# Another hand-written order for a two-layer attention and feed-forward kernel

## The reference, cut to what matters

```python
x = x + L0_xattn(layernorm(x), ctx)   # A: 16 heads of 16, softmax over 77 keys, output projection
x = x + L0_ffn(layernorm(x))          # B: 256 -> 1024 -> 256, ReLU; expert 0 alone counts; inner layernorm Y
x = x + L1_xattn(layernorm(x), ctx)   # C: one head of 256, softmax over 77 keys
x = x + L1_ffn(layernorm(x))          # D: token s goes through matrix W[idx[s]], idx = argmax of a table of 8 scores
...
idx = argmax(einsum('sp,tp->st', pe, sign(tile_sigs)))
out = take_along_axis(einsum('bsd,tod->bsto', x, W) + b, idx)
```

## Time and profile before

| | |
|---|---|
| median of the timed runs | 274.63 us (3 runs, 273.89 to 274.74) |
| span of the profiled execution, first to last instruction | 272.0 us |
| median less that span: what lies around the span | 2.6 us |
| PE busy | 249.2 us, 92% |
| DVE / POOL / ACT busy | 220.3 / 189.7 / 160.7 us |
| PE in the chain that ended last | 68% |
| mean granted TensorE clock | 0.982 of full speed |

### The profile page before, as it was taken

One profiled execution on the slowest core, in us unless ns is written; L12 is line 12 of the kernel. 1 busy time (PEld: TensorE's weight loads), 2 busy tenths in 40 slices (PEclk: granted clock), 3 DMA queues, 4 the chain that ended last, 5 costly groups with the idle time before them and its releaser, 6 DMA issues.

```text
span 272.0 us, 6214 instructions
## 1 busy us (share of the span) xinstructions
PE 249.2 (92%) x2048; PEld 221.2 (81%) x2048; DVE 220.3 (81%) x573; ACT 160.7 (59%) x510; POOL 189.7 (70%) x361
## 2 busy tenths in 40 slices
...
GB/s 175 329 326 89 0 81 0 2 39 42 39 2 40 41 265 86 14 9 2 0 2 63 76 77 42 58 60 40 57 217 2 0 0 2 0 2 2 39 154 116
DMA packets 11156, 17.61 MB, mean 65 GB/s; under 512 B 1377, under 2 KB 7509, under 8 KB 11125
## 3 DMA queue, kind: packets, MB, share of 16 engines
...
...
## 4 chain that ended last, share of the span: by engine, by line
PE 68%; DVE 15%; POOL 5%; ACT 5%; issue 4%; DMA 1%; SPq 0%; POOLq 0%; DVEq 0%; ACTq 0%
PE PB L266 29%; PE PB L259 12%; PE PB L464 9%; PE S L387 5%; PE PB L339 5%; PE PB L399 4%; PE S L377 4%; ACT E L1066 2%; DVE SX L659 2%; POOL E L1263 1%; DMA WKV<-in_w_k 1%; DVE SX L673 1%; POOL SM L1220 1%; DVE HL L686 1%; DVE XTL L638 1%
## 5 line engine op out<-in xcount | busy, mean ns | idle before, releaser
L1263 POOL TENSOR_TENSOR E<-E,SX 128x308 f32<-128x308 f32 x64 | 43.8, 712 | 10.7 <-DVE SX L676 10.4
L1066 ACT ACTIVATE E<-S,SX 128x77 f32<-128x77 f32 x128 | 39.4, 336 | 10.6 <-DVE SX L659 10.6
L266 PE MATMUL PB<-XTH,W1H 128*128 128x256 f32 x128 | 37.7, 295 | 1.5 <-DVE XTL L638 1.4
L266 PE MATMUL PB<-W2H,HH 128*128 128x256 f32 x128 | 37.6, 294 | 0.0
L266 PE MATMUL PB<-XTL,W1H 128*128 128x256 f32 x128 | 36.2, 283 | 0.0
L266 PE MATMUL PB<-XTH,W1L 128*128 128x256 f32 x128 | 36.2, 282 | 0.0
L266 PE MATMUL PB<-W2H,HL 128*128 128x256 f32 x128 | 35.5, 278 | 0.0
L266 PE MATMUL PB<-W2L,HH 128*128 128x256 f32 x128 | 35.5, 278 | 0.0
L1220 POOL TENSOR_TENSOR SM<-SM,nhalf 128x2 f32<-128x2 f32 x40 | 28.3, 707 | 3.1
L1089 ACT ACTIVATE HH<-PB 128x512 fp32r<-128x512 f32 x32 | 19.0, 598 | 18.0 <-PE PB L266 18.0
L1076 ACT ACTIVATE EW<-S 124x640 f32<-124x640 f32 x32 | 21.9, 711 | 10.9 <-PE S L387 10.1
...
## 6 DMA issues: line engine op xcount, KB each, us to landing
...
```

The source lines that it names most:

```text
L266: t = e.matmul(dst, a, b, start=first and j == 0, stop=last and j == n - 1)
L1066: t = e.activation(Ei[:, h * NK:(h + 1) * NK], P[:, at:at + NK], ACT.Exp, bias=SX[:, i, 0, k:k + 1], accum_out=SX[:, i, 1, k:k + 1])
L1263: t = e.tensor_tensor(Eh, Eh, SX[:, i, 2, 8 * a + h:8 * a + h + 4].unsqueeze(2).to_broadcast([128, 4, NK]), ALU.mult)
```

## The change

All four lists are written anew and most PSUM banks are other ones. The steps themselves, 246 on PE, 274 on DVE, 218 on ACT and 142 on POOL, are the same, with the same operations and waits; SP's list is untouched. The diff below is cut to the places that the text comes to. In the lists, `r_pairs` and the registers' `starts` stand later, `pivot` on DVE stands later, and `sx(1)` on POOL stands ahead of `en(6, 1, 1)`.

```diff
# PE
-            sc(2, 1, 0, 1); sc(2, 1, 1, 0); pv(1, 1); r_perm(1); w1(0, 0, 3); wo(1, 0); w1(0, 1, 2); w1(0, 2, 1)
-            w1(0, 3, 3); f_m(0); tE(2, 0, 0, 0); tA(3, 2); w2(0, 0, 0, 1); tE(2, 0, 1, 1); tB(1, 0); w2(0, 0, 1)
-            w2(0, 1, 0); q(3, 2); w2(0, 1, 1); w1(1, 0, 3); sc(3, 0, 0, 1); sc(3, 0, 1, 0); w1(1, 1, 0); w1(1, 2, 2)
...
-            cp(1, 3); cs(2, 0); tE(5, 1, 0, 1); tE(5, 1, 1, 0); co(1); pv(5, 0, 2); pv(5, 1); sc(6, 0, 0, 1)
-            sc(6, 0, 1, 0); wo(5, 2); tC(3, 0); tB(4, 3); sc(6, 1, 0, 0); q(7, 1); sc(6, 1, 1, 1); cp(2, 3); cs(3, 2)
-            co(2); w1(4, 0, 1); w1(4, 1, 0); w1(4, 2, 3); w1(4, 3, 2); cp(3, 1); tE(6, 0, 0, 1); tE(6, 0, 1, 0)
-            w2(4, 0, 0, 3); tB(5, 0); co(3); sc(7, 0, 0, 0); sc(7, 0, 1, 1); w2(4, 0, 1); w2(4, 1, 0); w2(4, 1, 1)
-            w1(5, 0, 1); w1(5, 1, 0); tE(6, 1, 0, 0); w1(5, 2, 2); tE(6, 1, 1, 1); w1(5, 3, 3); sc(7, 1, 0, 1)
...
-            pr(0, 0, 2); w2(6, 0, 0, 1); cp(4, 0); w2(6, 0, 1); tB(7, 3); co(4); w2(6, 1, 0); tC(5, 0); w2(6, 1, 1)
-            cs(5, 3); w1(7, 0, 2); tD(2, 1); w1(7, 1, 3); w1(7, 2, 0); w1(7, 3, 1); cp(5, 3); w2(7, 0, 0, 2); co(5)
-            tD(3, 0); w2(7, 0, 1); w2(7, 1, 0); w2(7, 1, 1); tC(6, 0); tD(4, 3); pr(0, 1, 1); cs(6, 2); pr(0, 2, 3)
...
+            tB(0, 0); wo(1, 1); sc(3, 0, 0, 1); w1(0, 0, 0); w1(0, 1, 2); f_c(); w1(0, 2, 0); w1(0, 3, 1)
+            tE(2, 0, 1, 0); w2(0, 0, 0, 2); sc(3, 0, 1, 0); sc(3, 1, 0, 1); w2(0, 0, 1); tB(1, 0); w2(0, 1, 0)
+            w2(0, 1, 1); tE(2, 1, 0, 0); w1(1, 0, 0); tA(4, 1); tE(2, 1, 1, 0); w1(1, 1, 3); sc(3, 1, 1, 0)
...
+            tA(6, 2); sc(5, 0, 0, 0); sc(5, 0, 1, 1); w2(2, 0, 0, 3); q(6, 1); cp(0, 2); w2(2, 0, 1); tE(4, 0, 1, 0)
+            w2(2, 1, 0); w2(2, 1, 1); tE(4, 1, 0, 0); tC(1, 1); co(0); tB(3, 0); tE(4, 1, 1, 1); cs(1, 3)
...
+            sc(7, 0, 0, 0); sc(7, 0, 1, 1); tC(3, 0); co(1); w2(4, 0, 1); cs(3, 0); cp(2, 1); tB(5, 3); w2(4, 1, 0)
+            tE(6, 0, 1, 0); cp(3, 3); co(2); co(3); w2(4, 1, 1); w1(5, 0, 1); tE(6, 1, 0, 1); w1(5, 1, 0)
+            tE(6, 1, 1, 1); pv(6, 0, 2); pv(6, 1); sc(7, 1, 0, 0); sc(7, 1, 1, 1); w1(5, 2, 3); wo(6, 1)
+            w1(5, 3, 0); tE(7, 0, 0, 1); w2(5, 0, 0, 2); tE(7, 0, 1, 1); w2(5, 0, 1); w2(5, 1, 0); w2(5, 1, 1)
...
+            w1(7, 1, 0); w1(7, 2, 2); cp(5, 1); w1(7, 3, 3); w2(7, 0, 0, 0); co(5); w2(7, 0, 1); w2(7, 1, 0)
+            w2(7, 1, 1); tD(3, 2); tC(6, 3); pr(0, 0, 1); tD(4, 3); cs(6, 2); pr(0, 1, 0); pr(0, 2, 3); cp(6, 2)
# DVE
-            hl(0, 3); apply("B", 1); lo("A", 3); r_pairs(); lo("B", 1); ssum(2, 1, 1); ql(3); y(0); stats("A", 4)
...
-            smax(5, 0, 0); ssum(4, 0, 1); lo("B", 3); ssum(4, 1, 0); cm(0); ssum(4, 1, 1); apply("C", 1); starts()
...
+            smax(2, 1, 0); smax(2, 1, 1); lo("B", 0); r_index(); ssum(2, 0, 1); f_q(); hl(0, 0); smax(3, 0, 0)
+            x1(1); ssum(2, 1, 0); hl(0, 1); kbl(1); stats("B", 1); stats("A", 4); hl(0, 2); hl(0, 3); apply("B", 1)
+            stats("A", 5); ssum(2, 1, 1); smax(3, 0, 1); ssum(3, 0, 0); smax(3, 1, 0); lo("B", 1); apply("A", 4)
...
+            hl(1, 2); ssum(3, 0, 1); apply("C", 0); ssum(3, 1, 0); hl(1, 3); ql(4); r_pairs(); ssum(3, 1, 1)
...
+            lo("A", 6); smax(5, 0, 0); hl(2, 3); ssum(4, 1, 0); stats("A", 7); ssum(4, 1, 1); stats("B", 3); ql(6)
+            starts(); apply("B", 3); apply("C", 1); smax(5, 0, 1); y(2); ssum(5, 0, 0); stats("Y", 2); apply("A", 7)
...
+            ssum(6, 1, 1); x3_(1); apply("B", 5); ssum(7, 0, 0); cm(3); lo("B", 5); x3_(2); smax(7, 0, 1); x3_(3)
# ACT
-            starts(); hi("A", 4); o(2); ex(3, 1, 0); ex(3, 1, 1); apply("C", 0); et(3, 0, 0); apply("A", 5)
...
+            hh(4, 2); hh(4, 3); starts(); ex(6, 1, 1); apply("B", 5); xtc(3); ex(7, 0, 0); hi("B", 5); cex(3)
# POOL
-            be(4); b2(4); bs(4); bs(5); en(6, 0, 0); rs("B", 5); bo(7); en(6, 0, 1); bs(6); bs(7); en(6, 1, 0); b2(5)
-            en(6, 1, 1); be(5); sx(0); rs("Y", 4); sx(1); rs("C", 4); rs("D", 0); sx(3); en(7, 0, 0); en(7, 0, 1)
...
+            rs("Y", 3); bo(6); rs("C", 3); b2(4); be(4); en(6, 0, 1); rs("B", 5); bs(6); en(6, 1, 0); one(5); sx(1)
+            bo(7); b2(5); en(6, 1, 1); en(7, 0, 0); be(5); sx(0); rs("Y", 4); sx(2); sx(3); one(6); en(7, 0, 1)
```

More of the change, by code:

```diff
@@ L532, in tensor @@
[L532 to L536, removed]
@@ L958, in f_o @@
                                 .to_broadcast([NK, 2, 256]), ALU.add).then_inc(s["d_f"], 1)
[L960 to L963, removed]
@@ L969, in vector @@
[L969 to L973, removed]
@@ L979, in vector @@
[L979 to L988, removed]
@@ L989, in vector @@
-            apply("D", 4); y(7); stats("Y", 7); x2(7); stats("C", 7); cm(6); pa(0, 1); apply("C", 7); pa(0, 2)
-            apply("D", 5); pa(0, 3); cm(7); x3_(6); stats("D", 6); x3_(7); apply("D", 6); stats("D", 7); apply("D", 7)
-            pa(1, 0); pa(1, 1); pa(1, 2); pa(1, 3); pa(0, 4); pa(1, 4); pa(0, 5); pa(1, 5); pa(0, 6); pa(1, 6)
-            pa(0, 7); pa(1, 7)
+            setup(); stats("A", 0); mask(); apply("A", 0); wq_lo(); kf(); lo("A", 0); stats("A", 1); kbl(0)
+            stats("A", 2); ql(0); apply("A", 1); vs(); smax(0, 0, 0); r_sign(); smax(0, 0, 1); apply("A", 2)
@@ new lines, in vector @@
+            f_stats(); smax(0, 1, 0); lo("A", 1); ssum(0, 0, 0); f_norm(); ssum(0, 0, 1); smax(0, 1, 1); ql(1)
+            vb(0); ssum(0, 1, 0); smax(1, 0, 0); lo("A", 2); stats("A", 3); ssum(0, 1, 1); r_ranks(); pivot(1)
+            pivot(2); ssum(1, 0, 0); smax(1, 0, 1); ql(2); f_kv(0); smax(1, 1, 0); smax(1, 1, 1); r_expert()
+            apply("A", 3); ssum(1, 0, 1); smax(2, 0, 0); ssum(1, 1, 0); vb(1); f_kv(1); lo("A", 3); ssum(1, 1, 1)
+            x1(0); ssum(2, 0, 0); r_position(); stats("B", 0); smax(2, 0, 1); f_m(); apply("B", 0); ql(3)
@@ new lines, in vector @@
+            smax(4, 0, 0); x1(2); apply("A", 5); stats("B", 2); f_o(); stats("A", 6); smax(4, 0, 1); y(1)
+            apply("B", 2); stats("Y", 1); smax(4, 1, 0); lo("A", 5); lo("B", 2); ssum(4, 0, 0); apply("A", 6); cm(0)
+            smax(4, 1, 1); x1(3); hl(2, 0); x2(1); ql(5); hl(2, 1); stats("C", 1); ssum(4, 0, 1); hl(2, 2)
+            lo("A", 6); smax(5, 0, 0); hl(2, 3); ssum(4, 1, 0); stats("A", 7); ssum(4, 1, 1); stats("B", 3); ql(6)
+            starts(); apply("B", 3); apply("C", 1); smax(5, 0, 1); y(2); ssum(5, 0, 0); stats("Y", 2); apply("A", 7)
@@ new lines, in vector @@
+            x3_(0); smax(5, 1, 0); lo("B", 3); x2(2); smax(5, 1, 1); cm(1); ssum(5, 0, 1); hl(3, 0); hl(3, 1)
+            stats("C", 2); x1(4); hl(3, 2); ssum(5, 1, 0); stats("B", 4); lo("A", 7); ssum(5, 1, 1); hl(3, 3)
+            apply("B", 4); smax(6, 0, 0); smax(6, 0, 1); apply("C", 2); y(3); lo("B", 4); ssum(6, 0, 0)
+            stats("Y", 3); x2(3); smax(6, 1, 0); ql(7); stats("C", 3); hl(4, 0); cm(2); ssum(6, 0, 1); x1(5)
+            ssum(6, 1, 0); apply("C", 3); stats("B", 5); hl(4, 1); smax(6, 1, 1); hl(4, 2); hl(4, 3); smax(7, 0, 0)
@@ new lines, in vector @@
+            ssum(6, 1, 1); x3_(1); apply("B", 5); ssum(7, 0, 0); cm(3); lo("B", 5); x3_(2); smax(7, 0, 1); x3_(3)
+            ssum(7, 0, 1); y(4); stats("Y", 4); hl(5, 0); x2(4); smax(7, 1, 0); hl(5, 1); stats("C", 4)
+            smax(7, 1, 1); stats("D", 0); stats("D", 1); hl(5, 2); ssum(7, 1, 0); hl(5, 3); x1(6); ssum(7, 1, 1)
+            stats("B", 6); apply("D", 0); apply("C", 4); apply("B", 6); y(5); stats("Y", 5); x2(5); lo("B", 6)
+            stats("C", 5); apply("D", 1); cm(4); stats("D", 2); hl(6, 0); hl(6, 1); hl(6, 2); apply("C", 5)
@@ new lines, in vector @@
+            apply("D", 2); stats("D", 3); hl(6, 3); x1(7); stats("B", 7); apply("B", 7); x3_(4); lo("B", 7); cm(5)
+            y(6); stats("D", 4); apply("D", 3); stats("Y", 6); hl(7, 0); hl(7, 1); x2(6); hl(7, 2); hl(7, 3)
+            stats("C", 6); x3_(5); stats("D", 5); apply("C", 6); y(7); stats("Y", 7); apply("D", 4); x2(7)
+            stats("C", 7); cm(6); pa(0, 0); apply("C", 7); pa(0, 1); pa(0, 2); x3_(6); cm(7); stats("D", 6)
+            apply("D", 5); pa(0, 3); apply("D", 6); x3_(7); stats("D", 7); pa(1, 0); apply("D", 7); pa(1, 1)
@@ new lines, in scalar @@
+            apply("B", 1); hi("B", 1); apply("A", 4); ex(3, 0, 1); et(2, 1, 0); et(2, 1, 1); hh(1, 0); hi("A", 4)
+            hh(1, 1); ex(3, 1, 0); hh(1, 2); hh(1, 3); qh(4); o(2); apply("C", 0); et(3, 0, 0); et(3, 0, 1)
+            et(3, 1, 0); ex(3, 1, 1); apply("A", 5); ex(4, 0, 0); xtc(0); et(3, 1, 1); o(3); apply("B", 2)
+            hi("A", 5); hi("B", 2); ex(4, 0, 1); ex(4, 1, 0); hh(2, 0); ex(4, 1, 1); qh(5); hh(2, 1); et(4, 0, 0)
+            apply("A", 6); hh(2, 2); hi("A", 6); hh(2, 3); cex(0); ex(5, 0, 0); qh(6); apply("C", 1); cpt(0)
```

112 lines of the change are left out of this document (54 added, 58 removed).

## The result

The changed kernel takes 295.24 us (median of 4 runs, 293.41 to 297.9) against 274.28 us beside it: a ratio of 1.0739, with an interval of 1.0696 to 1.0782. The forecast was slower, to 278.5 us, and 283.5 at most. The direction was right, and the added time is five times the forecast.

A forecast was written before the change was run, and what follows sets the result against it. PE was taken as the bound, 92% busy and full from 102 to 224 us, with DVE pacing the front. Terms summed to +3.9 us; 272.0 + 3.9 + 2.6 gave 278.5 us, range 273.0 to 283.5.

The forecast's parts named there:

- Lead at the front: At w1(1,0), moving r_pairs back frees lo(B,1) earlier and PE has more work done by then: -5.0 us.
- Two of its own signs of being wrong: Listed signs included the front's lead gone before 82 us, or granted clock at 0.50 anywhere behind 30 us.
- DVE's loads: DVE's starts() now stands ahead of apply(B,3) and apply(C,1), so PE waits at tC(1,1): +2.3 us.
- ACT's loads: ACT's register loads now stand ahead of ex(6,1,1) and xtc(3), so PE waits at cs(3,0) and cp(3,3): +1.6 us.
- POOL's gather: sx(1), ahead of en(6,1,1), waits for all four stores, so PE waits at tE(6,1,1,1): +6.2 us.
- Clock: The stop at tE(6,1,1) may drop PE's clock to its lower level; an eighth of 3.35 taken: +0.4 us.
- Knock-on: Late rs(Y,4) on POOL delays x2(4) and holds DVE, which catches up elsewhere: 0 us, from -1 to +3.
- All other places: Everything else in lists and banks trades places where PE is full before and after: costed at nothing.
- Tail: pr(0,0) and a tD move behind the last w2, less half of a pa on DVE: -1.6 us.
- the much slower one: Rival: the gap at tE(6,1,1) drops the clock (3.35) and POOL's queue stays behind (3): 284.4 us, chance 0.12.

The follow-up runs named there:

- e1_gather_back: The changed kernel with one POOL step, sx(1), put back behind rs(Y,4): 288.89 us, ratio 1.0529 to the kernel before.
- e5_front: The changed kernel's order and banks for the steps of its first 100 us, then the order of the kernel before: 279.70 us, ratio 1.0175 to the kernel before.
- e3_pairs_late: The kernel before with r_pairs moved behind smax(3,1,1) and ACT's starts() behind hh(3,3): 278.03 us, ratio 1.0125 to the kernel before.
- e9_lead_tail: e6_tail with the last seven instructions of r_pairs behind lo(B,1) and w1(1,1) ahead of sc(3,0,0): 273.46 us, ratio 0.9949 to the kernel before.
- e7_loads_in_stall: The changed kernel with both starts() moved into the time in which engines stand for POOL's gather: 288.02 us, ratio 1.0484 to the kernel before.
- e4_warm: The changed kernel with 54 identity transposes on PE ahead of tE(6,1,1,1), filling its pause: 296.02 us, ratio 1.0729 to the kernel before.
- e6_tail: The kernel before up to 203 us, then the remaining steps in the changed kernel's order and banks: 274.45 us, ratio 0.9977 to the kernel before.
- e10_pool_queue: The changed kernel with 13 POOL steps reordered, all four sx behind be(5), en(7,0,1) and rs(Y,4): 289.68 us, ratio 1.0498 to the kernel before.

## Why the prediction was wrong, step by step

The forecast's sum was +3.9 us of span, the measured one +20.6. Of the difference of 16.7 us, by the table of equal work:

- *Lead at the front, -5.0.* This is the step that failed. Over the front (to 96 of PE work) the kernel stands 3.5 us behind instead of 5.0 ahead: 8.5 of the 16.7, or 6.8 with e1_gather_back's profile of the same front. The step said: "35 x 0.11 = 3.9 us of work that came later before", and took that work as won. Work that is put ahead of a wait is won only as far as PE stood still; in 26.7 to 72.2 us PE had 3.86 us without work, and at the place 1.42, or 1.6 by the distance of starts (the earlier trace rows had the first number, the trace the others). What the place gave was 1.1 us here, 1.2 in e5_front, 1.7 in e3_pairs_late and e9_lead_tail. And the other steps of the front were costed at nothing "where PE is full before and after", which holds from 102 us on and not in the front, where the prediction itself has DVE pacing. By 36 of PE work 3.1 us were lost, 0.8 of them in waiting for the first weights; those 0.8 are not the order's, since e1_gather_back has the same list there, waits no longer than the kernel before (5.7 us) and stands 1.6 behind. Two of the waits there are 1.63 us at 30.7 (for DVE's `lo(A,2)`) and 1.53 us at 58.0 (for a maximum of group 2). They, `lo(B,1)` being 5.8 us late, and DVE's 43.04 busy us of 45.50 all say the same: DVE paces the front in either order, and the new one gives it `pivot`'s 2.9 us there, which the prediction cost at nothing with the rest. Two of its own signs of being wrong came: the lead was gone before 82 us, and the clock stood at 0.50 behind 30 us.
- *DVE's loads, +2.3: 3.0. ACT's loads, +1.6: 2.8.* Right in place and mechanism, 1.9 us short together. ACT's gap was taken at 3.7 us and is 4.49 in the trace. e7_loads_in_stall gives 7.0 us for both.
- *POOL's gather, +6.2: the wait is 7.0.* Right, and the cause is shown by e1_gather_back, in which this wait is gone.
- *Clock, +0.4: 2.7.* The clock fell as in the earlier trace rows and as the rival had it. That is what the Trainium skill's page "TensorE: Matmul & The Clock Gate" (section "HAM oscillation — how this bites in real kernels") says of long waits; here 7.04 us without a matmul were followed by 0.50. But e4_warm shows that the clock was not what had to be mended: with it at 1.00, PE waits for DVE and this stretch takes the same time.
- *Knock-on, 0: 2.7.* Mis-sized. In the trace `x2(4)`, at 202.20, comes behind 11.36 us in which DVE stands, until POOL's `rs(Y,4)` is done. "While PE stands for `en(6,1,1)`, the same time lets DVE catch up elsewhere" was wrong, since DVE is in order and stood too (0.00 busy from 192 to 202 us).
- *All other places, 0: 1.9. Tail, -1.6: -3.0 in the changed kernel and -0.6 by itself, between 0 and -1.3 (e6_tail).*

Of the rivals, the much slower one came nearest: it priced clock and queue at 3.35 and 3 us together, and they cost 2.7 each, 5.4. What its 284.4 us lacks is above all what the front lost.

What stays open: how the 4.9 us behind the gathers in e10_pool_queue are shared between waits and clock; what `pivot` costs by itself; and why the tail wins 3 us in the changed kernel and hardly any in e6_tail beyond the filling that is missing there.
